# A convolution block with two-expert routing: high and low parts of the weights side by side, element by element, in one tensor per layer

## The reference

```
scores = softmax(xn @ gate_w + gate_b)            # 4 experts
top_w  = softmax(two largest scores)
coef_e = sum of top_w[k] over the ranks k whose expert e occurs anywhere in the batch
hid_e  = relu(w1_e @ xn + b1_e)                   # 384 -> 384
y_e    = w2_e @ hid_e + b2_e                      # 384 -> 384
out    = x + sum over e of coef_e * y_e
```

## Time and profile before

| | |
|---|---|
| time, median of 3 runs | 2474.2 us (2473.63 to 2474.5) |
| time of the profiled execution | 2474.33 us |
| its span, first to last instruction | 2472.5 us |
| PE busy | 2451.0 us, 99% of the span |
| PEld busy | 2010.6 us, 81% |
| DVE busy | 1414.0 us, 57% |
| ACT busy | 465.4 us, 19% |
| share of PE in the chain that ended last | 98% |

### The profile page before, as it was taken

How to read it: one execution, slowest core, us unless ns; L and a number is a source line. 1 busy time by engine, 2 the same in 40 slices (tenths; PEclk the granted TensorE clock), 3 DMA queues, 4 the chain that set the end, 5 groups by cost and what they waited for, 6 DMA issues and landing times.

```text
span 2472.5 us, 27781 instructions
## 1 busy us (share of the span) xinstructions
PE 2451.0 (99%) x11372; PEld 2010.6 (81%) x11372; DVE 1414.0 (57%) x2952; ACT 465.4 (19%) x777; POOL 52.6 (2%) x36
## 2 busy tenths in 40 slices
PE   7999999999999999999999999999999999999999
PEld 5888888888888888888888888888888888888887
DVE  8656546556565565645564565546556564555443
ACT  3121111112111111111111121112112111121111
POOL 0000000000000000000000000000000000000000
PEclk9999999999999999999999999999999999999999
DMA  5223121321222113221322123121211222113110
GB/s 184 90 70 114 49 89 58 102 71 49 89 81 81 67 49 108 75 68 47 101 83 68 67 72 112 49 89 67 96 67 49 90 94 68 67 51 106 56 47 26
DMA packets 127520, 189.58 MB, mean 77 GB/s; under 512 B 16032, under 2 KB 80800, under 8 KB 127392
## 3 DMA queue, kind: packets, MB, share of 16 engines
q1 hardware_dynamic: 127392, 187.80, 22.4%
HBM read 146.03 MB, written 41.75 MB: 76 GB/s over the span
## 4 chain that ended last, share of the span: by engine, by line
PE 98%; DVE 2%; DMA 0%; issue 0%; POOL 0%; SPq 0%; ACT 0%; DVEq 0%; POOLq 0%
PE z_ps L430 16%; PE y_ps L449 16%; PE y_ps L451 16%; PE y_ps L450 16%; PE z_ps L432 16%; PE z_ps L431 16%; PE g_ps L300 1%; DVE w_lo L386 0%; DMA x_raw<-in_x 0%; DVE h_lo L488 0%; DVE x_raw L278 0%; DVE st L245 0%; DMA rows_dram<-wrow 0%; DVE hid L477 0%; DVE hid L474 0%
## 5 line engine op out<-in xcount | busy, mean ns | idle before, releaser
L477 DVE SCALAR_TENSOR_TENSOR hid<-z_ps,b_sb,rows 128x512 f32<-128x512 f32 x584 | 436.7, 748 | 901.9 <-PE z_ps L432 894.5
L449 PE MATMUL y_ps<-h_lo,w_hi 128*128 128x512 f32 x1764 | 687.2, 390 | 4.3 <-DVE h_lo L488 4.3
L451 PE MATMUL y_ps<-h_hi,w_hi 128*128 128x512 f32 x1764 | 686.9, 389 | 0.0
L450 PE MATMUL y_ps<-h_hi,w_lo 128*128 128x512 f32 x1764 | 686.8, 389 | 0.0
L430 PE MATMUL z_ps<-x_lo,w_hi 128*128 128x512 f32 x1740 | 680.9, 391 | 2.2 <-DVE hid L477 2.2
L432 PE MATMUL z_ps<-x_hi,w_hi 128*128 128x512 f32 x1740 | 677.4, 389 | 0.0
L431 PE MATMUL z_ps<-x_hi,w_lo 128*128 128x512 f32 x1740 | 676.8, 389 | 0.0
L484 ACT ACTIVATE h_hi<-hid 128x512 fp32r<-128x512 f32 x588 | 368.5, 631 | 1562.3 <-DVE hid L477 1553.4
L488 DVE SCALAR_TENSOR_TENSOR h_lo<-hid,h_hi 128x512 fp32r<-128x512 f32 x588 | 401.1, 682 | 8.3 <-ACT h_hi L484 7.1
L449 PEld LDWEIGHTS y_ps<-h_lo,w_hi 128*128 128x128 f32 x1764 | 331.5, 188 | 74.8 <-DVE h_lo L488 5.3
L430 PEld LDWEIGHTS z_ps<-x_lo,w_hi 128*128 128x128 f32 x1740 | 326.6, 188 | 78.8 <-issue 12.3
(11 more groups left out here) (88 smaller groups left out, 374.4 us busy)
## 6 DMA issues: line engine op xcount, KB each, us to landing
rows<-rows_dram SPq DMA_DIRECT2D x48, 1280.0 KB, 6.1
x_raw<-in_x SPq DMA_DIRECT2D x62, 588.0 KB, 5.9
res<-in_x SPq DMA_DIRECT2D x18, 768.0 KB, 5.6
out<-res SPq DMA_DIRECT2D x17, 768.0 KB, 4.3
rows_dram<-wrow SPq DMA_DIRECT2D x32, 98.0 KB
w_in<-in_w SPq DMA_DIRECT2D x3, 576.0 KB, 10.2
res<-in_x SPq DMA_DIRECT2D x2, 744.0 KB, 4.9
out<-res SPq DMA_DIRECT2D x2, 744.0 KB, 4.1
```

The lines of the kernel that those rows point to most:

```text
L449: nc.tensor.matmul(y, w2_hi[:, e, k, ms], h_lo[:, slot], start=first, stop=False)
L450: nc.tensor.matmul(y, w2_lo[:, e, k, ms], h_hi[:, slot], start=False, stop=False)
L451: ins = nc.tensor.matmul(y, w2_hi[:, e, k, ms], h_hi[:, slot], start=False, stop=last)
L477: nc.vector.scalar_tensor_tensor(hid[:, q % HIDS], z_ps[:, q % ZB], b1_sb[:, e, k:k + 1], coef, ALU.add, ALU.mult).then_inc(scaled, 1)
```

## The change

The four tensors become two. In each, the last dimension is a pair: first the high part of an element, then its low part. The old names become views of them, with every second element. So the 128 weights of a block that PE loads are now 8 bytes apart, with those of the other part between them; ACT's copies write, and DVE's subtractions read one input and write, with the same step. The loaded weights, the data that PE streams, sizes, slices, waits and all other tensors stay as they are.

```
-        w1_hi = sb("w1_hi", [P, E, NJ, HID], f32r)
-        w1_lo = sb("w1_lo", [P, E, NJ, HID], f32r)
-        w2_hi = sb("w2_hi", [P, E, NK, C], f32r)
-        w2_lo = sb("w2_lo", [P, E, NK, C], f32r)
+        w1_both = sb("w1_both", [P, E, NJ, HID, 2], f32r)
+        w2_both = sb("w2_both", [P, E, NK, C, 2], f32r)
+        w1_hi, w1_lo = w1_both[:, :, :, :, 0], w1_both[:, :, :, :, 1]
+        w2_hi, w2_lo = w2_both[:, :, :, :, 0], w2_both[:, :, :, :, 1]
```

## The result

The changed kernel takes 2541.45 us (4 runs, 2540.31 to 2542.89), against 2473.91 us before (4 runs). The ratio is 1.0274, with a 95% interval of 1.0261 to 1.0286: slower by 67.5 us.

A forecast was written before the change was run, and what follows sets the result against it. The prediction took PE as the bound: 10,584 matmuls at 226.7 ns, 2399 us of a 2472.5 us span, plus a start-up led by DVE. Its terms, 0 + 0 + 0, left the time at 2474 us, range 2469 to 2616.

The forecast's parts named there:

- what the loads take from the matmuls: PE's 10,584 matmul steps: strided loads could change each by up to 13.3 ns, +141 or -141 us; taken as +0.
- the 13.3 ns: Part of each 226.7 ns step over 213.3 ns for 512 columns at full clock; unexplained, possibly matmul reads giving way to loads.
- loads and matmuls taking turns: Rival on PE's steps: the 13.3 ns are load reads, with twice as many places now; 2615 us in full, chance 16%.
- its price: Taking turns on PE's steps at full size: +141 us, 2615 us, which set the range's upper end.
- The other steps: The weight loads' own rate, and ACT's copies with DVE's subtractions at the start; each taken as +0.
- about 295 was worked out: Row of a PE weight load in ns if the step halved its rate, against 188 before; matmul steps the same.
- hidden, as the prediction had it: PE's weight loads at half rate would still be ready 7 to 19 ns before the next matmul start, +0.
- the +0 that was taken: ACT's eight copies and DVE's eight subtractions in the start-up: between +0 and +20 us, taken as +0.

The follow-up runs named there:

- step 0: Kernel before, but each weight load reads the first of its 128 columns 128 times; 2523.7 us, mean step 231.5 ns.
- data_step_0_weights_8: Changed kernel's weights at 8 bytes, with each main-loop matmul streaming its first column 512 times; 2370.0 us, mean step 216.66 ns.
- step_8_shift_32: Changed kernel with its weights moved on by 32 bytes; 2568.8 us, mean step 236.05 ns.
- shift_128: Kernel before with its contiguous weights moved on by 128 bytes; 2535.3 us, ratio 1.0252.
- data_step_8: Weights as before, but high and low parts of the streamed x and h side by side, so matmuls stream at 8 bytes; 4838.9 us.
- shift_64: Kernel before with its contiguous weights moved on by 64 bytes; 2542.3 us, mean step 233.33 ns.
- shift_96: Kernel before with its contiguous weights moved on by 96 bytes; 2551.9 us, ratio 1.032.
- step_16: Parts of both layers' weights side by side, four to an element, a step of 16 bytes; 2569.3 us, mean step 235.0 ns.

## Why the prediction was wrong

The forecast was no change; the kernel became 2.7% slower.

The step that failed is the one on what the loads take from the matmuls: "I take +0: the steps stay at 226.7 ns whatever DVE, ACT and the transfers do in the long middle". That argument doesn't bear on the question. It is about other engines; the load and the stream are both PE's. It measured +6.67 ns a step, +68 us, half of the 13.3 ns that the prediction had as the bound. And the sign was there to be read: the nine steps of 231 ns behind each gate product in the trace of before show that contiguous loads can cost more than 226.7 ns. I had read one settled stretch.

The rival of that kind, loads and matmuls taking turns, had the sign, the range and the look of the profile (longer steps at full clock, 426.7 ns still at half clock), with 16%. Its reason for the size was wrong, so it was partly luck that the range held the time through its price. It took the 13.3 ns for reads of the load and doubled them with the memory that a load spans. The runs show that 10 of the 13.3 go away when the stream reads one place, and that the loss doesn't follow the count of a load's places (step 0: 231.5; 64-column loads: 229.8). What they show in its place: the strided loads cost only beside a stream that reads many places (no loss with `data_step_0_weights_8`), and the step is that of a rhythm of load and stream, which differs with the place of the weights and, in `step_8_shift_32` and `shift_128`, from one restart to another. Over the places tried, without that of before, contiguous weights have 232.7 to 234.3 ns and strided ones 230.0 to 236.1 in the mean. So what the change lost is the rhythm of 226.7 ns, which contiguous weights had at one of five places and strided ones at none of four; a price of the step of 8 bytes beside that is not shown.

What the Trainium skill's "SBUF — State Buffer" (section "Door 1: The DMA port swizzle") and "Advanced Engine Details and Errata" (section "SBUF Cachelines") state about lines, two hits on a 16-byte line for full speed, nearly holds for the rate of the loads here (row 193 against 188 ns). It doesn't hold for the stream: `data_step_8` has two floats on a line and runs at half speed (451.2 against 226.67 ns). The Trainium skill's port of its own for weights, in "TensorE: Matmul & The Clock Gate" (section "Step-by-step: what each phase is for"), doesn't keep load and stream apart here either: moving the weights alone by 32 bytes takes the steps from 226.67 to 233.33 ns.

The other steps held. The loads kept nearly their rate at 8 bytes (188 to 193 ns). About half the rate came at 16 bytes, with a row of 310 ns where about 295 was worked out. Whether it was hidden, as the prediction had it, is open: the stream, by the estimate of 226 ns, fills the step, and the 1.7 ns by which 235 ns are over the change are no more than a place can make. ACT's copies rose by at most 0.13 us each, DVE's subtractions by at most 0.02 us, and the start is not longer, which is the +0 that was taken.

Open: what load and stream share, why 226.7 ns are reached at one place alone, and what picks the rhythm at a restart. The shifts of contiguous weights also moved all tensors behind them by 64 or 128 bytes; that this alone does nothing was not tried. But `shift_64`, `shift_96` and `shift_128` move them by the same 128 bytes and have three different steps, and the streamed tensors lie ahead of the weights and stay.

## What to carry to other kernels

When PE streams float32r without a pause, a few nanoseconds a matmul can hang on the address of the weights, and on the rhythm that load and stream fall into after an interruption. A layout change that moves neither work nor waits can cost or give 3%, so try a few offsets, each more than once, before blaming the layout, and look at the steps right behind an interruption as well as at the settled ones. Keep the streamed operand contiguous: there a step of 8 bytes doubled the time.

## What the runs showed of the hardware that was not expected

- A step of 8 bytes doubles the time of a matmul on the streamed side (226.67 to 451.2 ns) and hardly touches the load (row 188 to 193 ns). The load's row grows only from 8 to 16 bytes, to 310 ns, and no further at 64 bytes (299 to 303).
- One program, with everything in its place, had steps of 240.0 ns in some stretches between gate products and 232.1 in others (`step_8_shift_32`).
- Of 13.3 ns a step over 512 columns, 3.3 remain when the stream reads one place (215, 215 and 220 ns in turn).
- A row of a load can grow by 65%, to 310 ns, while the steps grow by 4% (`step_16`).
- ACT's copy and DVE's subtraction of 1152 elements take 1.26 and 1.36 us at a step of 8 bytes, but in `step_16` 2.29 and 2.25 us.
